# Graph and expert network on one Trainium2 core: splitting a tile into two f16 parts before its transposes instead of after them

## What is computed

```python
x = x + gnn(layernorm(x), src, dst, ...)
x = x + ffn(layernorm(x), ...)          # two of eight experts, chosen for the whole batch

def gnn(x, rows, cols, W_in, b_in, Wl, bl, Wg, bg, gamma, beta):
    dinv = rsqrt(degree(rows) + 1)[:, None]
    h = x @ W_in + b_in
    for l in range(4):
        msg = segment_sum((h * dinv)[cols], rows) * dinv
        global_ctx = mean(h, axis=0) @ Wg[l] + bg[l]
        z = relu((h + msg) @ Wl[l] + bl[l] + global_ctx)
        h = (z - mean(z)) * rsqrt(var(z) + 1e-5) * gamma[l] + beta[l]
    return h
```

## Time and profile before

| | us |
|---|---|
| median of three runs | 3125.68 (3124.12 to 3125.77) |
| profiled execution, its own time | 3126.55 |
| its span, first to last instruction | 3124.9 |
| TensorE busy | 2998.0 (96%) |
| VectorE busy | 1943.2 (62%) |
| ScalarE busy | 949.0 (30%) |
| mean granted TensorE clock | 0.977 of full speed |

### The profile page before, as it was taken

One profiled execution on the slowest core, in us unless ns is written; L12 is line 12 of the kernel. 1 busy time (PEld: TensorE's weight loads), 2 busy tenths in 40 slices (PEclk: granted clock), 3 DMA queues, 4 the chain that ended last, 5 costly groups with the idle time before them and its releaser, 6 DMA issues.

```text
span 3124.9 us, 55195 instructions
## 1 busy us (share of the span) xinstructions
PE 2998.0 (96%) x18038; PEld 1697.4 (54%) x18038; DVE 1943.2 (62%) x5237; ACT 949.0 (30%) x2112; POOL 78.0 (2%) x169
## 2 busy tenths in 40 slices
PE   6999996999999999999999999999999999988998
PEld 5777774444444444444444444444444444445776
DVE  8999997555555555555555555555566666666676
ACT  5898887111111111111111111111111111116765
POOL 0000000000000000000000000000000000000111
PEclk9999997999999999999999999999999999998999
DMA  4333325222222222122221222212222222211000
GB/s 132 89 87 88 88 82 139 77 85 85 92 79 82 85 79 71 63 71 72 72 72 62 72 72 72 71 63 71 74 84 78 78 84 84 84 38 43 23 25 26
DMA packets 138137, 233.87 MB, mean 75 GB/s; under 512 B 13717, under 2 KB 105988, under 8 KB 138018
## 3 DMA queue, kind: packets, MB, share of 16 engines
q1 hardware_dynamic: 131058, 217.55, 21.4%
q10 hardware_dynamic: 4608, 8.39, 0.8%
q0 software_dynamic: 2352, 6.40, 0.7%
HBM read 186.58 MB, written 45.74 MB: 74 GB/s over the span
## 4 chain that ended last, share of the span: by engine, by line
PE 83%; ACT 10%; DVE 4%; issue 3%; DVEq 0%; DMA 0%; ACTq 0%; SPq 0%; POOL 0%; POOLq 0%
PE bank L1647 66%; ACT tab L1270 8%; PE bank L1605 4%; PE bank L1749 4%; PE bank L1732 4%; PE bank L1595 1%; PE bank L1495 1%; DVE later L812 1%; PE bank L1515 1%; DVE region L779 1%; PE bank L1541 1%; ACT later L1294 0%; PE bank L1535 0%; PE bank L1745 0%; ACT xnb L1288 0%
## 5 line engine op out<-in xcount | busy, mean ns | idle before, releaser
L1647 PE MATMUL bank<-tab,region 128*128 128x512 f16 x9604 | 2142.0, 379 | 17.3 <-DMA region<-adjacency 17.3
L1647 PEld LDWEIGHTS bank<-tab,region 128*128 128x128 fp8e4 x9604 | 940.5, 98 | 1067.6 <-DVE tab L896 19.6
L1270 ACT ACTIVATE tab<-later 128x539 fp8e4<-128x539 uint8 x588 | 336.1, 674 | 1.9 <-DVE later L812 1.9
L779 DVE TENSOR_SCALAR region<-iota_w,src_col,src_w 128x540 bf16<-128x540 int16 x858 | 310.4, 413 | 0.4 <-issue 0.2
L1373 ACT ACTIVATE sd<-mv,eps_c 128x1 f32<-128x1 f32 x196 | 57.7, 295 | 811.2 <-DVE mv L1011 811.2
L1004 DVE SCALAR_TENSOR_TENSOR region<-bank,c_back,later 128x256 f32<-128x256 f32 x196 | 94.8, 484 | 331.5 <-PE bank L1605 331.5
L995 DVE TENSOR_TENSOR region<-bank,region 128x256 f16<-128x256 f32 x196 | 83.2, 425 | 287.4 <-ACT region L1369 287.4
L1369 ACT ACTIVATE region<-bank 128x256 f16<-128x256 f32 x196 | 75.3, 384 | 567.5 <-PE bank L1595 567.5
L1367 ACT ACTIVATE region<-bank 128x256 f32<-128x256 f32 x196 | 75.3, 384 | 305.4 <-PE bank L1647 305.4
L1605 PE MATMUL bank<-later,region 128*128 128x256 f16 x1176 | 160.7, 273 | 0.9 <-DVE region L995 0.9
L1337 ACT ACTIVATE tab<-region,c_write 128x256 f32 (+1 forms) x147 | 74.7, 508 | 268.6 <-DVE region L1020 268.6
(11 more groups left out here) (235 smaller groups left out, 2421.1 us busy)
## 6 DMA issues: line engine op xcount, KB each, us to landing
region<-adjacency SPq DMA_DIRECT2D x196, 784.0 KB, 4.3
adjacency<-tab SPq DMA_DIRECT2D x12, 3136.0 KB, 13.9
region<-in_x POOLq DMA_DIRECT2D x48, 128.0 KB, 2.3
out<-region SPq DMA_DIRECT2D x48, 128.0 KB, 1.7
tab<-in_x SPq DMA_DIRECT2D x5, 1024.0 KB, 11.9
dstf<-in_L_ffn_W ACTq DMA_DIRECT2D x16, 256.0 KB, 2.6
srcf<-in_L_ffn_W ACTq DMA_DIRECT2D x16, 256.0 KB, 2.9
tab<-in_L_ffn_W SPq DMA_DIRECT2D x4, 512.0 KB, 4.9
```

Of the source, the lines that this page charges most:

```text
L779: v.tensor_scalar(hot_s[:, j, :], iota_w[:, 0:WP], src_col[:, ds(first_block[0] + j, 1)], src_w[:, ds(first_block[0] + j, 1)], ALU.is_equa ...
L1270: ins = a.activation(stage[h][:, :, slot, f * LANES:f * LANES + n], counts[:, :, 0:n], ACT.Copy, saturate=False)
L1647: ins = mm(acc[a][:, :], A_s[:, a, m, :], tab[:, here + m, :], start=m == 0, stop=m == T - 1)
```

## The change

U is split into its two f16 parts while it still has rows as rows. ScalarE writes the high part to `Ux[:, 0]` (Ux is a f16 view of U's second tile), VectorE the difference to `Ux[:, 1]`. TensorE makes four f16 transposes, two for each part, into one bank read as f16; one ScalarE copy of 128x512 moves both parts to `uT`. The turn moves from matmul 14 to 19 of the next tile, the product from 24 to 28. `ident_h` is a f16 copy of the identity, made once. In ScalarE's program the copy to f16 stands behind a wait for U and one for the turn before.

```diff
--- before.py
+++ after.py
@@ -77,7 +77,7 @@
 TINY = 1e-15
 SCAN = 512
 TURN_AT, PRODUCT_AT = 0, 8
-BEFORE_T, BEFORE_MM = 14, 24
+BEFORE_T, BEFORE_MM = 19, 28
 
 
 def hold(eng, sem, value):
@@ -212,6 +212,7 @@
         A32_s = Abuf.bitcast(I32).rearrange("p (a w) -> p a w", a=RING + 1)
         AG_s = Abuf.bitcast(BF16).rearrange("p (a m s) -> p a m s", m=T, s=P)
         U = work(RING * D).rearrange("p (a f) -> p a f", f=D)
+        Ux = U[:, 1, :].bitcast(F16).rearrange("p (a f) -> p a f", f=D)
         uT = work(D).bitcast(F16).rearrange("p (a k n) -> p a k n", k=KC, n=P)
         at[0] += (RING + 1) * D
 
@@ -235,6 +236,7 @@
         rep = sb("rep", [P, P, WIN], F16)
         iota_w = sb("iota_w", [P, W], I16)
         ident = sb("ident", [P, P])
+        ident_h = sb("ident_h", [P, P], F16)
         mean_w = sb("mean_w", [P, P])
         mean_last = sb("mean_last", [P, P])
         ones = sb("ones", [P, P])
@@ -313,6 +315,7 @@
         fbet = sb("fbet", [P, D])
 
         bank = [ctx.enter_context(nc.psum_tensor(f"bank{i}", [P, 512], F32)) for i in range(8)]
+        uT_bank = bank[3][:, 0:D].bitcast(F16).rearrange("p (a k n) -> p a k n", a=2, k=KC)
         T3 = [bank[i][:, 0:D].rearrange("p (k n) -> p k n", k=KC) for i in range(8)]
         acc = [bank[0], bank[1], bank[2], bank[7]]
 
@@ -382,7 +385,8 @@
         u_ready = sem("u_ready")
         uT_done = sem("uT_done")
         uT_copied = sem("uT_copied")
-        uT_split = sem("uT_split")
+        u_high = sem("u_high")
+        u_split = sem("u_split")
         wl_in = sem("wl_in")
         wmax_set = sem("wmax_set")
         wsum_done = sem("wsum_done")
@@ -685,6 +689,8 @@
             own.done(v.memset(eps_c[:], EPS))
             own.done(v.memset(before[:], 0.0))
 
+            dve.wait_ge(const_set, 1)
+            own.done(v.tensor_copy(ident_h[:], ident[:]))
             dve.wait_ge(edges_in, 96)
             v.tensor_copy(rawf[:], raw_dst[:]).then_inc(raw_cast, 1)
             dve.wait_ge(raw_cast, 1)
@@ -991,8 +997,8 @@
                     late = last and a < RING
                     if late:
                         moments(t - 1)
-                    dve.wait_ge(uT_copied, n + 2)
-                    v.tensor_tensor(uT[:, 1, :, :], T3[3], uT[:, 0, :, :], ALU.subtract).then_inc(uT_split, 1)
+                    dve.wait_ge(u_high, n + 1)
+                    v.tensor_tensor(Ux[:, 1, :], U[:, 0, :], Ux[:, 0, :], ALU.subtract).then_inc(u_split, 1)
                     if first and a in (1, 2):
                         dve.wait_ge(scan_in[a - 1], i * 16 + 16)
                         v.tensor_reduce(w_lim[:, ds(i + (a - 1) * 2 * EX, 1)], scan_s[a - 1], AX, ALU.max,
@@ -1251,7 +1257,7 @@
 
 
             act.sem_inc(scan_done, 2)
-            for s in (staged, words_ready, uT_copied, uT_split, g_words, g_staged):
+            for s in (staged, words_ready, uT_copied, uT_done, g_words, g_staged):
                 act.sem_inc(s, 1)
 
 
@@ -1365,8 +1371,11 @@
                 def step(n, t, i, s):
                     act.wait_ge(agg_done, n + RING + 1)
                     a.activation(lo_f[:, s, :], acc[s][:, D:2 * D], ACT.Copy).then_inc(lo_ready, 1)
+                    act.wait_ge(u_ready, RING + n + 1)
                     act.wait_ge(uT_done, n + 1)
-                    a.activation(uT[:, 0, :, :], T3[3], ACT.Copy).then_inc(uT_copied, 1)
+                    a.activation(Ux[:, 0, :], U[:, 0, :], ACT.Copy).then_inc(u_high, 1)
+                    act.wait_ge(uT_done, n + 2)
+                    a.activation(uT, uT_bank, ACT.Copy).then_inc(uT_copied, 1)
                     if last and s < RING:
                         spread(t - 1)
                     act.wait_ge(var_ready, n + 1)
@@ -1588,17 +1597,17 @@
 
 
             def turn_u(n):
-                pe.wait_ge(u_ready, RING + n + 1)
-
-                pe.wait_ge(uT_split, n + 1)
-                for k in range(KC):
-                    ins = nc.tensor.transpose(T3[3][:, k, :], U[:, 0, k * P:(k + 1) * P], ident[:])
+                pe.wait_ge(u_split, n + 1)
+                pe.wait_ge(uT_copied, n + 1)
+                for b in range(2):
+                    for k in range(KC):
+                        ins = nc.tensor.transpose(uT_bank[:, b, k, :], Ux[:, b, k * P:(k + 1) * P], ident_h[:])
                 ins.then_inc(uT_done, 1)
 
             def product_u(n, l):
                 if l == 0:
                     pe.wait_ge(wx_ready, 1)
-                pe.wait_ge(uT_split, n + 2)
+                pe.wait_ge(uT_copied, n + 2)
 
                 parts = [(a, b, k) for a, b in ((0, 0), (0, 1), (1, 0)) for k in range(KC)]
                 for q, (a, b, k) in enumerate(parts):
```

## The result

The changed kernel took 3133.33 us in the median of nine runs (3131.14 to 3135.98), the kernel before 3125.77 (3124.12 to 3132.46). The ratio is 1.0021, with a 95% interval of 1.0013 to 1.0030: slower by 6.6 us, with 4.1 to 9.4 us as bounds (the two medians by themselves lie 7.6 us apart). The forecast was 3134.7, the range 3130 to 3146. The times show that the kernel is slower; what the loss is made of is read from the traces, which are of one execution each.

What follows compares the result with a forecast made beforehand. TensorE's aggregation matmuls were taken to bound the kernel. Transposes 0.6, edges 2.4, boundaries 5.2 and tail 1.2 made +9.4 us, less 0.4 for first turns: +9.0 on the 3125.68 median, 3134.7 us; range 3130 to 3146.

Steps and rivals of the forecast that it cites:

- The steady tile: Middle of a layer: 11.45 us a tile, TensorE never stopping; four f16 transposes add 0.003 a tile, +0.6 us over 196.
- Readiness: Before each turn: U's f16 parts ready 8.84 us after the product's start, 9.17 at a VectorE loop edge; turn at 9.28.
- Parts have to be there 0.19 us before the turn: At the turn: lead the transposes need over ready parts, taken from a layer's first turn; makes loop edges 0.08 us late.
- The term of 2.4 us for the edges: VectorE's loop edges, one tile in three, layers 1 and 2: 30 turns each 0.08 us late; bounds 0 and 6 us.
- The boundaries: Three layer ends: later product lengthens waits at the next layer's first aggregation (+0.87) and the mean (+0.86): +5.2 us.
- The tail: Last tile, without cover: copy, subtract held by `moments`, and transposes delay the product by 1.05; `normal` ends later: +1.2 us.
- Pair floor: At the turn: f16 transposes held to a floor per load and matmul, +21 us more (3156) or 3177; chance 0.10.
- Clock: At layer boundaries: waits of 1.0 and 1.2 us lower TensorE's clock, 2.5 us each, +7.5, 3142; chance 0.08.
- Late at each tile: Inside tiles: hand-overs 0.2 us longer, 100 tiles stall 0.1, edges 0.3; 16 us more, 3151; chance 0.07.
- Not slower: At the turn: transposes run below the column rate, saving 21.6 us, which outweighs the 9: 3113; chance 0.05.
- Cover enough: Inside tiles: edges cost nothing, transposes slightly less than now; boundaries and tail remain, +6 or below, 3131; chance 0.15.

## Why the prediction was right, and where its size was off

**The steady tile: right.** The period stayed at 11.45 to 11.46; 0.6 us was put to it in all, and it costs 0.9. Transposes were put at 0.056 and are 0.056; the doubled ones show it alone. The rule of 81 ns in the Trainium skill (page TensorE: Matmul & The Clock Gate, section Back-to-back issue gap) would have made 0.32 us of the four; the trace has 0.22, so here the figure of about 56 ns that the page gives for an isolated matmul holds in a real stream too.

**Readiness: right to 0.01 us, but its margin was wrong.** The parts were forecast for P + 9.17 at an edge. The subtract in the timeline ends at 1204.97 with the product of that tile at 1195.80 (1205.09 less 9.29): P + 9.17. The 0.01 is in part luck, since errors of 0.03 cancel: U was ready at P + 8.17 instead of 8.20, and from there to the parts it took 1.00 instead of 0.97, with a shorter copy and longer hand-overs. "Parts have to be there 0.19 us before the turn" is the step that failed. It came from one row, a blocked turn with f32 loads of 0.14 us, two waits and the register work of a loop's first tile. In the changed kernel the edges have 0.10 to 0.12 from the subtract to the turn and lose nothing, and where the turn comes too early, at 18, it starts 0.06 behind the subtract. Which part of the old row made it 0.19 (the loads, the waits or the loop's start) no run takes apart. The term of 2.4 us for the edges is near zero: of the 0.9 us found inside the tiles, 0.6 was put to the transposes, and the rest is below what these rows can tell. This is nearly all of the difference between 9.0 and 6.7. The runs' times by themselves could not have told the two apart, since their interval, 4.1 to 9.4, holds both.

**The boundaries: right.** Forecast 3 x 1.73 less 0.4, 4.8; measured 4.9. The old kernel with the new slots shows them without the split (4.7), the version with its own slots for tile 0 takes one of the two away, and the later slots make both grow by 1.24 to 1.29 us for six matmuls where the clock stays, 1.30 by the 0.2159 of one. These two waits come from the slots and not from the split: at 15 and 22, with `moments` behind the split, the product is even earlier than in the kernel before. But the early slots have a wait of their own there, at the first turn of the loop (0.74, 0.75 and 0.24 us), and its rows name the split's subtract as the releaser.

**The tail: right in kind**, 1.1 against 1.2. That `normal` sets it, as forecast, shows in the run with turn 18. The clock falls in the tails too, which the forecast did not have; it moves this term by up to 0.4 us from run to run, so the closeness is in part luck.

**The rivals.** Pair floor: refuted by the doubled transposes. Clock: granted 1.00 at the boundaries of the changed kernel, but it fell at two waits of 2.14 us in the kernel with the later slots. Late at each tile: did not happen. Not slower: the transposes are at the column rate and not below it. Cover enough (chance 0.15): true of the edges, which were free, and not of the transposes, which take no less than before; the result, 6.6 us, lies nearer to its 6 than to the 9.0 of the sum.

## What to carry to other kernels

In a program order written out by hand, two numbers may cost more than the operations that they place. Where work of the tile before is slotted into the stream of the next, the steady tile stays the same as long as the parts are ready at the turn, while the boundary pays for every matmul by which the product is late. So put the slots as early as the slowest variant of the loop allows (here the last layer, with `moments` in front of the split) and move that variant's other work behind. The first turn behind a boundary is such a variant too: at 15 it had to wait for the parts. And take the margin for "ready" from a row of the same kind of load and wait.

## What the runs showed of the hardware that was not expected

At VectorE's loop edges in the changed kernel the first weight load of the turn started 0.05 us behind the end of the subtract (1205.02 against 1204.97), after 0.26 us in which the load queue was idle, and the first transpose still came at its usual P + 9.29. Idle time of the loads was not idle time of the matmuls there.

An idle time of 2.14 us in front of a layer brought the clock down to 1.2 GHz twice in one execution, three and five matmuls behind its end, while 1.98 us in front of a layer and 2.17, 2.32 and 2.33 us in front of the mean in the same execution did not. In the last tile of the kernel before, 2.05 us idle, two transposes and 0.94 us idle were enough. So the length of one wait doesn't decide it; what does, these runs leave open.
